# Graph convolution on one core: chunks of ten tiles instead of twelve, in a ring of 21 instead of 18

## What is computed

```python
h = jnp.maximum(_layernorm(x, axis=-1), 0.0)
x_i = h[dst]
x_j = h[src]
feat = jnp.concatenate([x_i, x_j - x_i], axis=-1)
m = jnp.maximum(feat @ W1 + b1, 0.0) @ W2 + b2
out = jax.ops.segment_max(m, dst, num_segments=12500)
return x + jnp.where(jnp.isneginf(out), 0.0, out)
```

## Time and profile before

| | us |
|---|---|
| runs of before | 4085.41, 4079.10, 4081.74; median 4081.74 |
| profiled execution, its own time | 4073.29 |
| span of the profiled execution | 4071.5 |
| POOL busy in the span | 3053.3 (75%) |
| PE busy in the span | 2888.8 (71%) |
| DVE busy in the span | 2410.9 (59%) |
| ACT busy in the span | 850.4 (21%) |

### The profile page before, as it was taken

How to read it: one execution, slowest core, us unless ns; L and a number is a source line. 1 busy time by engine, 2 the same in 40 slices (tenths; PEclk the granted TensorE clock), 3 DMA queues, 4 the chain that set the end, 5 groups by cost and what they waited for, 6 DMA issues and landing times.

```text
span 4071.5 us, 47102 instructions
## 1 busy us (share of the span) xinstructions
PE 2888.8 (71%) x14651; PEld 1613.3 (40%) x14651; DVE 2410.9 (59%) x7589; ACT 850.4 (21%) x3260; POOL 3053.3 (75%) x3189
## 2 busy tenths in 40 slices
PE   3200099999878887878887877787887877887820
PEld 2100055555444444444444444444444444444410
DVE  5110188888666666666666666666666666666631
ACT  4420032222112212112112112112112112112100
POOL 5777777777777777777777777777777777777767
PEclk8555599999999999999999999999999999999955
DMA  9993133333333333333333333333333333333331
GB/s 372 378 414 147 37 101 105 107 107 104 82 85 85 82 85 86 81 86 86 81 85 85 84 83 85 82 85 86 81 85 85 82 84 86 81 85 85 85 85 47
DMA packets 198940, 443.48 MB, mean 109 GB/s; under 512 B 61989, under 2 KB 66658, under 8 KB 187946
## 3 DMA queue, kind: packets, MB, share of 16 engines
q1 hardware_dynamic: 54890, 219.23, 16.3%
q0 software_dynamic: 103312, 109.12, 12.9%
q10 hardware_dynamic: 40487, 112.13, 7.4%
HBM read 222.67 MB, written 217.71 MB: 108 GB/s over the span
## 4 chain that ended last, share of the span: by engine, by line
POOL 63%; issue 20%; PE 12%; DVE 2%; DMA 1%; ACT 1%; ACTq 0%; POOLq 0%; DVEq 0%; SPq 0%
POOL rows L382 58%; PE ps_g L680 10%; POOL a_edges L405 2%; POOL a_rows L438 2%; PE ps_m L699 2%; PE ps_t L690 1%; DMA blocks<-in_dst_dram,blk_idx 1%; ACT zt L456 0%; ACT shared L483 0%; DMA b_table<-shared 0%; DVE state L915 0%; PE ps_m L641 0%; DVE shared L784 0%; DVE stat L788 0%; DVE stat L782 0%
## 5 line engine op out<-in xcount | busy, mean ns | idle before, releaser
L382 POOL DMA_INDIRECT rows<-b_table,src_idx x2868 | 2740.7, 956 | 874.1 <-issue 873.2
L680 PE MATMUL ps_g<-shared,dst_all 128*128 128x512 bf16 x9509 | 2216.6, 389 | 84.7 <-DVE dst_all L944 84.4
L680 PEld LDWEIGHTS ps_g<-shared,dst_all 128*128 128x128 bf16 x9509 | 936.4, 101 | 1178.5 <-DVE dst_all L944 110.7
L887 DVE SCALAR_TENSOR_TENSOR a_fill<-a_fill,keep 128x64 f32<-128x64 f32 x3125 | 875.3, 280 | 173.9 <-DMA a_fill<-a_edges 154.6
L915 DVE SCALAR_TENSOR_TENSOR state<-state,keep,ps_m 128x64 f32<-128x64 f32 x3125 | 862.5, 276 | 83.7 <-PE ps_m L699 64.4
L901 DVE TENSOR_TENSOR rows<-rows,a_fill 128x512 f32<-128x512 f32 (+1 forms) x521 | 270.5, 560 | 1022.8 <-DMA rows<-b_table,src_idx 1022.5
L699 PE MATMUL ps_m<-w_diag,zt 128*128 128x128 f32 x3126 | 496.2, 318 | 498.1 <-ACT zt L565 494.2
L699 PEld LDWEIGHTS ps_m<-w_diag,zt 128*128 128x128 f32 x3126 | 446.4, 223 | 609.0 <-ACT zt L565 597.4
L543 ACT ACTIVATE dst_all<-ident_h,key_octet 128x128 f16<-128x128 f16 x257 | 102.7, 400 | 2421.5 <-DVE state L915 2421.1
L553 ACT ACTIVATE dst_all<-ps_g,dst_all 128x64 f32<-128x64 f32 x2056 | 450.0, 344 | 0.0
L690 PE MATMUL ps_t<-ident,rows 128*128 128x128 f32 x1563 | 216.1, 275 | 230.3 <-DVE rows L901 230.3
(11 more groups left out here) (116 smaller groups left out, 446.6 us busy)
## 6 DMA issues: line engine op xcount, KB each, us to landing
a_edges<-rows SPq DMA_DIRECT2D x80, 1250.0 KB, 14.8
a_fill<-a_edges SPq DMA_DIRECT2D x260, 384.0 KB
states<-state ACTq DMA_DIRECT2D x260, 384.0 KB, 2.4
rows<-b_table,src_idx POOLq DMA_INDIRECT x2868, 2.4
a_fill<-b_table ACTq DMA_DIRECT2D x12, 256.0 KB, 8.9
shared<-in_x_dram SPq DMA_DIRECT2D x5, 560.0 KB
b_table<-shared ACTq DMA_DIRECT2D x5, 560.0 KB
a_table<-a_rows ACTq DMA_DIRECT2D x1, 2800.0 KB
```

What stands on the lines that cost most here:

```text
L382: nc.gpsimd.indirect_dma_start(out=rows[:, c % RING, t * C:(t + 1) * C], out_offset=None, in_=b_table, in_offset=at(src_idx[:, q % SRC_RIN ...
L680: last = nc.tensor.matmul(ps_g[:, half, :], key_is[:, half, g, :], table[:, g, t, :], start=(g, t) == (0, 0), stop=g == PAGES - 1)
L887: nc.vector.scalar_tensor_tensor(here, before, flag(c, 0, t), here, ALU.mult, ALU.add).then_inc(fill_step, 1)
```

## The change

Three constants. A chunk becomes 10 tiles: 312 chunks and again a tail of 5 tiles. From the fourth chunk on nine tiles are gathered and one is picked. The ring has 21 slots of 10 tiles (210 tiles, before 216); 17 chunks are gathered ahead of the scatter. All else follows from these by the formulas of the kernel: the group of `add`, relu and W2 behind the first eight tiles has two tiles instead of four, the choose stands ahead of fill 8 instead of fill 10, and the DMAs for `a_fill` and `states` carry 320 KB instead of 384 KB.

```diff
-    CHUNK = 12
-    RING = 18
+    CHUNK = 10
+    RING = 21
...
-    PREFIX = 14
+    PREFIX = 17
```

## The result

The changed kernel takes 4002.45 us (median of five runs, 4000.42 to 4004.07), the kernel before 4079.10 us beside it (4074.22 to 4085.41). The ratio is 0.9819, with a 95% interval of 0.9808 to 0.9830: 1.8% faster, some 74 us (69 to 78 us by the interval). The profiled execution took 4003.74 us, with a span of 4001.9 us; its span is 69.6 us under that of before.

The account below looks back on a forecast made before the run. The prediction took GpSimd's unbroken stream of gathers as the bound: -65.1 us for 52 gathers, -3 for the later stage, -1.3 at the end, -69.4 us from the 4081.74 us median, say 4012.5 us; range 4003 to 4022 us.

Follow-up runs that it names:

- the next size down: Chunks of eight tiles, ratios to the kernel before: every eighth chunk without a pick, add in pieces, 0.9939; every sixth without a pick, add whole, 0.9814.

## What to carry to other kernels

When one engine issues a stream that is never held, count its instructions: the price of one, times those that a change removes, gave 65 of the 69.6 us by which the profiled span shrank, though the work went to an engine that is 78% busy. Before moving more, price the engine that receives it by its step in order, waits included: a step without its filler stood 2.8 us, and the next size down came out 49 us behind in one form and level in the other. Where a mean duration differs between stages, look for what stands beside the single long instructions before calling it a property of the stage.

## What the runs showed of the hardware

- A gather's instruction on GpSimd takes 0.944 us. One that starts while VectorE executes an instruction with two SBUF operands (sum or fill) lasted up to 1.48 us: with over 0.3 us still to run, as in the additions, it lasted longer by that time less 0.13 us. Gathers that start during an instruction with at most one SBUF operand, of up to 1.9 us, keep their 0.944 us, and so do those that start first. 312 more sums of 0.68 us cost 47.7 us, 312 reductions of one operand of 1.0 us 7.6 us, none of it in gathers that started during the reduction. With the sum cut into pieces back to back the longest such gather fell from 1.46 to 1.07 us; the time didn't change.
- The kernel before took 4072 to 4083 us on some chips and 4787 to 4825 us on others. On the latter, signals of PE reached ACT, DVE and GpSimd together and late, 7 us behind the transposes in the step shown and 1.9 us behind the end of GpSimd's last gather of the chunk, and the delay was gone with the last gather of the run. The ratio of two kernels is another there.
- PE's granted clock was 1.00 from 1,700 to 3,700 us in the changed kernel. Before it was 0.94 from 1,100 to 3,800 us, where W2 matmuls behind 1.91 us of idle time took 2.59 us, against 1.50 us in the stage without idle time.
